# Two relative blocks: the mixture's first steps made inside the attention, the attention's parts two slots sooner, and the last batch's second normalization inside the mixture

## The reference, cut to what matters

```
x = x + 0.5 * routed_ffn(layernorm(x))        # stage 1
x = x + retention(layernorm(x))               # stage 2
x = x + 0.5 * routed_ffn(layernorm(x))        # stage 3
x = x + 0.5 * L1_ffn(layernorm(x))            # stage 4
x = x + plain_attention(layernorm(x))         # stage 5
x = x + 0.5 * L1_ffn(layernorm(x))            # stage 6

L1_ffn(src):
    x  = layernorm(src);  q, k, v = x @ wq, x @ wk, x @ wv          # 16 heads of 8
    att = softmax((q.k + q.p[relative position]) * scale)           # p = pe @ wp
    src = src + (att @ v) @ wo
    x2  = layernorm(src)
    sel = sigmoid(x2 @ sel_w)                                       # 32 experts
    gate = sel where it is among the token's top 4, else 0
    h   = relu(x2 @ keys[e]);   out = sum over e of gate[e] * (h @ values[e])
    return src + out
```

## Time and profile before

| what | us |
|---|---|
| median of 3 runs | 3079.71 (3077.35 to 3080.72) |
| the profiled execution: its own time | 3079.54 |
| its span, first to last instruction | 3077.7 |
| mean granted TensorE clock | 0.965 of 2.4 GHz |
| f4m, first issue of SP to f4m gate load | 1452.7 to 1458.2 |
| f6m, first issue of SP to the end of the span | 2696.7 to 3077.7 |

### The profile page before, as it was taken

How to read it: one execution, slowest core, us unless ns; L and a number is a source line. 1 busy time by engine, 2 the same in 40 slices (tenths; PEclk the granted TensorE clock), 3 DMA queues, 4 the chain that set the end, 5 groups by cost and what they waited for, 6 DMA issues and landing times. The chain is left out here.

```text
span 3077.7 us, 62307 instructions
## 1 busy us (share of the span) xinstructions
PE 2832.4 (92%) x21152; PEld 2287.9 (74%) x21152; DVE 1974.7 (64%) x4490; ACT 1863.7 (61%) x5065; POOL 2052.6 (67%) x2634
## 2 busy tenths in 40 slices
PE   6999798799969999997999998998999999979999
PEld 4888576588858888886788865665888888768887
DVE  5544486544448888886555556775788888755554
ACT  2233344233359999997444446776999999844444
POOL 4223574322158888884899984555788888679998
PEclk9999898899979999998999998998999999989999
DMA  3000464000022221121555546552121221055554
GB/s 112 1 1 1 104 141 102 1 1 1 1 51 42 53 53 42 43 45 46 210 191 193 193 162 127 114 117 47 43 42 43 57 49 43 22 207 200 197 195 166
DMA packets 152507, 266.08 MB, mean 86 GB/s; under 512 B 14098, under 2 KB 124946, under 8 KB 129138
## 3 DMA queue, kind: packets, MB, share of 16 engines
q1 hardware_dynamic: 152194, 262.11, 30.2%
HBM read 204.06 MB, written 53.67 MB: 84 GB/s over the span
## 5 line engine op out<-in xcount | busy, mean ns | idle before, releaser
L3005 POOL TENSOR_TENSOR f4m_ht_lo<-f4m_ht,f4m_ht_hi 128x512 fp32r<-128x512 f32 x256 | 330.6, 1309 | 36.6 <-ACT f4m_ht_hi L2941 28.5
L3005 POOL TENSOR_TENSOR f6m_ht_lo<-f6m_ht,f6m_ht_hi 128x512 fp32r<-128x512 f32 x256 | 329.8, 1303 | 31.3 <-ACT f6m_ht_hi L2941 22.0
L2980 DVE SCALAR_TENSOR_TENSOR f6m_ht<-f6m_hr,f6m_gate 128x512 f32<-128x512 f32 x256 | 176.3, 691 | 164.6 <-PE f6m_hr L2868 158.9
L2980 DVE SCALAR_TENSOR_TENSOR f4m_ht<-f4m_hr,f4m_gate 128x512 f32<-128x512 f32 x256 | 175.7, 690 | 160.2 <-PE f4m_hr L2868 149.4
L2941 ACT ACTIVATE f4m_ht_hi<-f4m_ht 128x512 fp32r<-128x512 f32 x256 | 161.3, 632 | 191.1 <-DVE f4m_ht L2980 189.5
L2941 ACT ACTIVATE f6m_ht_hi<-f6m_ht 128x512 fp32r<-128x512 f32 x256 | 161.5, 632 | 188.1 <-DVE f6m_ht L2980 188.0
L2518 ACT ACTIVATE f4a_pr<-f4a_sr,f4a_nm 128x256 f32<-128x256 f32 x512 | 241.0, 486 | 30.3 <-DVE f4a_nm L2593 30.2
L2518 ACT ACTIVATE f6a_pr<-f6a_sr,f6a_nm 128x256 f32<-128x256 f32 x512 | 241.1, 486 | 30.1 <-DVE f6a_nm L2593 30.0
L2708 POOL TENSOR_TENSOR f4a_rr<-f4a_tmp 128x256 f32<-128x256 f32 x256 | 187.2, 731 | 87.6 <-DVE f4a_tmp L2601 85.8
L2708 POOL TENSOR_TENSOR f6a_rr<-f6a_tmp 128x256 f32<-128x256 f32 x256 | 187.2, 731 | 79.3 <-DVE f6a_tmp L2601 77.2
L2601 DVE TENSOR_TENSOR f4a_tmp<-f4a_ur,f4a_turn 128x512 f32<-128x512 f32 x256 | 174.9, 684 | 67.3 <-PE f4a_ur L2378 63.9
(11 more groups left out here) (490 smaller groups left out, 9417.0 us busy)
## 6 DMA issues: line engine op xcount, KB each, us to landing
f4m_gate<-f4m_gates SPq DMA_DIRECT2D x64, 1024.0 KB, 4.6
f6m_gate<-f6m_gates SPq DMA_DIRECT2D x64, 1024.0 KB, 4.7
r_scratch<-r_parts SPq DMA_DIRECT2D x32, 192.0 KB, 2.2
all_qs<-r_scratch SPq DMA_DIRECT2D x16, 384.0 KB, 4.9
all_ks<-r_scratch SPq DMA_DIRECT2D x16, 384.0 KB, 6.7
f4al_scratch<-f4a_parts SPq DMA_DIRECT2D x32, 192.0 KB, 2.2
all_qs<-f4al_scratch SPq DMA_DIRECT2D x16, 384.0 KB, 4.8
all_ks<-f4al_scratch SPq DMA_DIRECT2D x16, 384.0 KB, 6.8
```

The lines of the kernel that those rows point to most:

```text
L2980: nc.vector.scalar_tensor_tensor(ht[:, n % RB, :], hr[:, n % HB, :], 0.0, gate[:, q % GB, n % LOADED, :], ALU.max, ALU.mult).then_inc(ht_r ...
L3005: nc.gpsimd.tensor_tensor(ht_lo[:, n % RB, :], ht[:, n % RB, :], ht_hi[:, n % RB, :], ALU.subtract)\
```

## The change

1. A class `Opening` is made once per relative block, ahead of the attention. It holds what the end of the attention and the start of the mixture share: the room for weight chunks 0 and 1, the rounded and low parts of keys chunk 0 and of the even groups' tokens, the gates' copy, the small tiles of the second normalization, and the semaphores of all of it. The mixture takes its semaphores over.
2. In the attention SP fetches chunks 0 and 1 right behind the last batch's read. In step B+1 PE turns the gates of group 0 at slot 14 into the bank of the relating products, ACT copies them at slot 15, SP stores them; POOL at slot 13 rounds keys chunk 0 and the first group's tokens (before: ACT) and makes their low part. In step B+2 DVE makes the keys' low part at slot 2.
3. The mixture starts with the gate load. ACT's first work is values chunk 0.
4. The last batch (`kept(e)` is false for it) gets no normalization from POOL's root on in the attention. The root stands at the start of POOL's list in the mixture, the normalized tokens behind ACT's first split; PE turns them behind expert 2 and selects behind expert 5; ACT takes the tokens at n = 2 and the exponential at n = 5; DVE does the five steps of the gates at n = 8, 10, 11, 13 and 14.
5. The rest of the heads moves to slot 13 of the start step, the second part to slot 15 of it, the third part to slot 1 of the prepare step. For f6's batch 1, which stage 5 has started, the first two stand at slot 0 of the prepare step.
6. For room, the odd groups' gate copy and the late batch's tokens share the tile yt (with waits that keep them apart), and the second buffer of stage 5's pts lies in the opening's chunk room.

```diff
 relative_ffn:
+        opening = Opening(nc, Pool_(nc, ctx, f"{tag}o"), f"{tag}o", k, w, io, x2t, gates)
...
 relative_attention, SP:
                 lead.read(sp, i)
+            opening.fetch(sp)                 # chunks 0 and 1, two DMAs of 512 KB
             sp.wait_ge(stacked, B * LANDED)
+            opening.store_gates(sp)
 relative_attention, PE:
-                if n == AT["x2t"] and e:
+                if n == AT["x2t"] and e and kept(e):
+                    opening.turn_tokens(pe, e[0], x2, fill(it, "x2t")).then_inc(desk.filled, 1)
+                if n == AT["sel"] and e and kept(e):
+                    opening.select(pe, x2s, fill(it, "sel")).then_inc(desk.filled, 1)
+                if n == 14 and it[0] == B + 1:
+                    pe.wait_ge(ur.emptied, 2 + B * H)
+                    opening.turn_gates(pe, ur.psum[:, 0, :])
 relative_attention, ACT:
-                if n == 3 and p:
-                    lead.second_part(act, p[0])
+                if n == 15 and b:
+                    lead.second_part(act, b[0])
+                if n == 0 and p and led and p[0] == 1:
+                    lead.second_part(act, 1)
...
+                if n == 15 and it[0] == B + 1:
+                    opening.take_gates(act, ur.psum[:, 0, :])
 relative_attention, DVE:
+                    if n == 2 and i == B - 1:
+                        opening.low_part(dve)
-                    if n == 15:
-                        gate_sum(it)
+                    if n == 15 and kept(e):
+                        dve.wait_ge(desk.emptied, desk.done(it, "sel"))
+                        opening.gate_sum(dve, i)
...
-            for n in sorted(GATES):
-                GATES[n](B - 1)
 relative_attention, POOL:
-                    if n == 1: ... lead.rest_of_heads(pool, p[0])
-                    if n == 3: lead.third_part(pool, p[0])
+                if b and n == 13:
+                    pool.wait_ge(desk.emptied, desk.done(it, "qk"))
+                    lead.rest_of_heads(pool, b[0])
+                if p and n == 0 and led and p[0] == 1:
+                    lead.rest_of_heads(pool, 1)
+                if p and n == 1:
+                    lead.third_part(pool, p[0])
+                if e and n == 7 and kept(e):
+                    opening.root(pool, e[0])
+                if n == 13 and it[0] == B + 1:
+                    opening.high_parts(pool)
 mixture, SP:
-            fetch(0)
-            fetch(1)
-            store_gates(0)
             load_gates(0)
 mixture, PE:
-            turn_gates(0)
...
+                if n == 2:
+                    opening.turn_tokens(pe, LATE, x2, turned[:, :]).then_inc(late_filled, 1)
+                if n == 5:
+                    pe.wait_ge(late_taken, 1)
+                    opening.select(pe, x2s, turned[:, :]).then_inc(late_filled, 1)
 mixture, ACT:
-            take_gates(0)
-            split_x(0)
-            split_weights(0)
             split_weights(1)
+            opening.normal(act, LATE, x2)
...
+                if n == 2:
+                    act.wait_ge(late_filled, 1)
+                    opening.take_tokens(act, LATE, x2s, turned[:, :]).then_inc(late_taken, 1)
+                if n == 5:
+                    act.wait_ge(late_filled, 2)
+                    opening.take_selection(act, LATE, turned[:, :]).then_inc(late_taken, 1)
 mixture, DVE:
-            rest_of_weights(0)
             rest_of_weights(1)
...
+                if n == 8:
+                    dve.wait_ge(late_taken, 2)
+                    opening.gate_sum(dve, LATE)
+                if n in GATES:                # {10: inverse, 11: best, 13: left, 14: kept}
+                    GATES[n](dve, LATE)
 mixture, POOL:
-            rest_of_x(0)
+            opening.root(pool, LATE)
 Opening:
+    def high_parts(self, pool):
+        pool.wait_ge(self.fetched[0], 16)
+        nc.gpsimd.tensor_copy(self.keys_hi[:, :, :], self.full[:, 0, :, :]).then_inc(self.weights_hi, 1)
+        pool.wait_ge(self.gates_ready, self.GT // TT)
+        nc.gpsimd.tensor_copy(self.x_hi ..., first).then_inc(self.x_hi_ready, 1)
+        pool.wait_ge(self.x_hi_ready, 1)
+        nc.gpsimd.tensor_tensor(self.x_lo ..., first, self.x_hi ..., ALU.subtract).then_inc(self.x_lo_ready, 1)
+    def low_part(self, dve):
+        dve.wait_ge(self.weights_hi, 1)
+        self.nc.vector.tensor_tensor(self.keys_lo[:, :, :], self.full[:, 0, :, :], self.keys_hi[:, :, :], ALU.subtract)
+    def take_tokens(self, act, i, x2s, bank):
+        for dst in (x2s, self.tiles[:, i, :]):
+            last = self.nc.scalar.activation(dst, bank[:, 0:T], ACT.Identity, scale=..., bias=...)
```

More of the change, by code:

```diff
@@ L1402, in relative_ffn @@
                 lead = Lead(nc, Pool_(nc, pair, f"{tag}l"), f"{tag}l", x_sb, k, w, io)
-                ahead(lead)
-            relative_attention(nc, f"{tag}a", x_sb, k, io, w, x2t, gates, lead)
-        mixture(nc, f"{tag}m", x_sb, k, io, x2t, gates, then, out=out)
+                ahead(lead, opening.full)
+            relative_attention(nc, f"{tag}a", x_sb, k, io, w, opening, lead)
+        mixture(nc, f"{tag}m", x_sb, k, io, x2t, gates, opening, then, out=out)
 class Forerun:
@@ L2277, in relative_attention @@
+def relative_attention(nc, tag, x_sb, k, io, w, opening, lead=None):
     x_b = x_sb[:, :, :].rearrange("p (b t) c -> p b t c", t=TT)
@@ L2339, in later_than, with kept @@
             return not isinstance(b[0], int) or b[0] >= first
+        def kept(e):
+            return e[0] < B - 1
         def run(step, ahead):
@@ L2445, in small @@
                     lead.project_heads(pe, b[0], fill(it, "qk")).then_inc(desk.filled, 1)
-                if n == AT["x2t"] and e:
-                    out = fill(it, "x2t")
-                    pe.wait_ge(x2_ready, e[0] * TT + TT)
-                    for t in range(TT):
-                        mm = nc.tensor.transpose(out[:, t * P:(t + 1) * P], x2[:, t, :], k.ident)
-                    mm.then_inc(desk.filled, 1)
-                if n == AT["sel"] and e:
-                    out = fill(it, "sel")
-                    for t in range(TT):
-                        mm = nc.tensor.matmul(out[:, t * E1:(t + 1) * E1], x2s[:, t * P:(t + 1) * P], w.selw[:, :],
-                                              start=True, stop=True)
-                    mm.then_inc(desk.filled, 1)
+                if n == AT["x2t"] and e and kept(e):
[5 more added lines that the diff above has]
+                    opening.turn_gates(pe, ur.psum[:, 0, :])
             def related(it, n):
@@ L2537, in small @@
                     lead.normal_source(act, b[0])
-                if n == 9 and e:
-                    act.wait_ge(s1_shift, e[0] + 1)
-                    for t in range(TT):
-                        nc.scalar.activation(x2[:, t, :], s1[:, t, :], ACT.Identity, scale=rstd3[:, t:t + 1], bias=nb3[:, t:t + 1])\
-                            .then_inc(x2_ready, 1)
+                if n == 9 and e and kept(e):
+                    opening.normal(act, e[0], x2)
                 if n == AT["xt"] and b:
@@ L2758, in _, with mixture @@
             run(step, shared)
-def mixture(nc, tag, x_sb, k, io, x2t, gates, then=None, out=None):
+def mixture(nc, tag, x_sb, k, io, x2t, gates, opening, then=None, out=None):
     G, GT, HB, RB, GB, SB = 8, 4, 4, 3, 2, 4
@@ L2768, in mixture @@
         a = Pool_(nc, ctx, tag)
-        full = a.sb("full", [P, SB, CHUNK, P])
-        halves = {name: (a.sb(f"{name}_hi", [P, E1, P], F32R), a.sb(f"{name}_lo", [P, E1, P], F32R))
-                  for name in ("keys", "values")}
-        (keys_hi, keys_lo), (values_hi, values_lo) = halves["keys"], halves["values"]
-        x_hi, x_lo = a.sb("x_hi", [P, 2, W], F32R), a.sb("x_lo", [P, 2, W], F32R)
+        a.sems, opening.a.sems = opening.a.sems, []
+        full = a.sb("full", [P, SB - 2, CHUNK, P])
@@ L2786, in mixture @@
+        (hr_filled, ht_ready, hi_ready, lo_ready, out_done, yt_ready, turn_done, x_done, late_filled, late_taken) = [a.sem(n) for n in (
+            "hr_filled ht_ready hi_ready lo_ready out_done yt_ready turn_done x_done late_filled late_taken").split()]
         stored = a.sem("stored")
-        fetched = [a.sem(f"fetched{n}") for n in range(SB)]
+        fetched = opening.fetched + [a.sem(f"fetched{n}") for n in range(2, SB)]
         gate_in = [a.sem(f"gate_in{n}") for n in range(GB)]
+        LATE = B - 1
@@ L2793, in mixture, with chunk_in, weights, chunk_of @@
         ORDER = {item: n for n, item in enumerate(CHUNKS)}
+        MADE = 2
+        def chunk_in(s):
+            return opening.full[:, s, :, :] if s < MADE else full[:, s - MADE, :, :]
+        def weights(name, part, e):
+            if name == "values":
+                return halves[name][part][:, e, :]
+            return (opening.keys_hi, opening.keys_lo)[part][:, e, :] if e < CHUNK else halves[name][part][:, e - CHUNK, :]
+        def chunk_of(name, part, c):
+            first = c - (CHUNK if name == "keys" else 0)
```

(7 more changed lines are left out.)

233 lines of the change are left out of this document (140 added, 93 removed).

## The result

The changed kernel takes 3056.39 us (median of 5 runs, 3054.97 to 3065.12), the kernel before in the same measurement 3080.27 us (3077.35 to 3083.13): ratio 0.9933 (this kernel's time over that of the kernel before), 95% interval 0.992 to 0.9946, which leaves out 1. The profiled execution has a span of 3054.2 us against 3077.7. So 23.5 us went, where 28.0 were forecast.

What follows compares the result with a forecast made beforehand. PE, busy 92% of the span, was taken as the bound, so only its waits and low-clock time could go. Moved parts -10.7 us, opening and late batch -17.3: together -28.0 from 3079.54, so 3051.5 us, range 3046 to 3057.

Steps and rivals of the forecast that it cites:

- Waits for stacks: In both attentions, PE's slot 11 waits for stacked heads all go: 5.45 us in f4, 6.10 in f6.
- A clean step stays 34.25: Attention steps without long PE waits keep 34.25 us, since idle time on POOL and ACT takes up the moved parts.
- Rivals 2, 3 and 5: 2: ACT slot 15 too full, 3064, 0.07; 3: lighter steps, 3043, 0.06; 5: POOL slot 13 delays terms, 3101, 0.02.
- The fill of f4: At f4's start batch 0's third part stands behind batch 1's root on POOL: 0.9 us later, bounds 0 to 1.5.
- Taken off the path, 24.1: Between attention and mixture, late-batch work and gate and key preparation leave the path: 12.2 us in f6, 11.9 in f4.
- 0.6 per block in the last steps: In the attention's last steps ACT's gates' copy adds 0.6 us per block, bounds 0 and 2.6.
- Rival 4: Gates reach memory late, with SP behind its waits for landed stacks; 5.44 us per block stay: 3062, chance 0.03.
- The first group, 2.8 per block: In the mixture's first group, added ACT and DVE work costs 2.8 us per block, bounds 0.5 and 4.6.
- Other edits cost nothing: Value chunk 0's split and rest stand beside the gate load; the other attention's second buffer only changes address: 0 us.
- rival 1: The opening gives half back: longer low clock, first group and last steps at upper prices; 3062.5, chance 0.12.

Runs made afterwards that it cites:

- the run without it: The changed kernel with the last batch's second normalization, turns and gates back in the attention, none of it in the mixture; ratio 0.9972 to the kernel before.
- the 224 bytes: The changed kernel with 224 unused bytes per partition behind the opening's tiles, bringing the mixture's tiles back to byte 160 of 256; ratio 0.9914 to the kernel before.
- the second measurement: The changed kernel itself, measured once more on another chip: 3058.4 us, ratio 0.9943 to the kernel before.

## Why the forecast held, and where it missed

- **Waits for stacks: right in mechanism, short in f6.** They are gone in every step. Thirteen steps of f4 are 5.9 us shorter (forecast 5.45), fourteen of f6 7.4 us (forecast 6.10). The forecast took 34.25 us for each of the fourteen, but the first of them needs only 33.4 where nothing waits, so the waits in f6 were more than it read. In timed runs the parts are worth less than in these traces: 5 us (2 to 8) alone and 7, with some 5 of doubt, when taken back. "A clean step stays 34.25": 34.24, by the place of the tiles. Rivals 2, 3 and 5 did not come: ACT's slot 15 and POOL's slot 13 carry the moved parts without a longer step.
- **The fill of f4: 0.9 forecast, 1.0 in this pair, but 1.6 over all traces** (nine with the new slots 68.5 to 69.5 us from PE's first instruction to the third batch's product for v, five with the old ones 67.2 to 67.8): above the upper bound of 1.5. The forecast put the cost ahead of PE's first relating product. Behind that product the stretch takes 48.6 to 48.8 us with the new slots and 47.6 to 47.9 with the old, 1.0 us that the forecast does not have; ahead of it 0.7 us come on average. Which instruction takes it was not followed.
- **Taken off the path, 24.1, less 0.6 per block in the last steps: right.** 22.9 us forecast, 23.2 measured. DVE closes batch 14's gates 0.69 and 0.66 us later, counted from PE's product for v of batch 15; the rest is gone. The late batch is 6.5 and 6.8 of it, the opening 5.2 and 4.7. Rival 4 did not come.
- **The first group, 2.8 per block: too dear.** The late batch costs 1.2 to 1.5 us by the run without it. Opening and late batch together cost 1.7 us by the averages above, and 0.9 by the pair of traces (1.7 less the place's 0.8); the stretch itself varies by 2 us between traces of kernels that are alike in it. The sum took ACT's and DVE's added work in full up to product 13, as in a serial loop. That a part of it lay beside other work is the likely reason, but not shown.
- **The failed step: "Other edits cost nothing".** The forecast says there that a moved buffer "only changes its address", and it has no term at all for where the tiles of the mixture lie: the tokens' tiles of the even groups and the first keys' tiles now begin at byte 160 of 256, all the others at 192. These places cost 3.13 us in the six periods of each block and 0.8 in its first group. With the 224 bytes these 7.8 us go. Between the two traces the mixtures differ by 8.7 us, since f6's last group took 1.35 us longer in the changed kernel's first trace than in its second.

The 4.5 us between forecast and trace are thus: periods +6.3, last groups +1.8, parts with both fills +1.5 (the clock in f6's start in it), first groups -2.2, last steps and passages -0.3, and ahead of f4 -2.6. A price that was too high and a higher clock ahead of f4 hid more than half of what the places cost. So that 3056.39 lies in the forecast's range, 0.6 us below its upper end, is in part luck. By the second measurement's ratio the kernel would stand at 3062 us (3058 to 3066), above the range. That is near rival 1's 3062.5, but rival 1's mechanism, a slower opening, is not what the runs show. The range itself is narrower than the bounds it names: added in full they give 3045 to 3060.

Not settled: what in the chip makes products slower. Shown is only this dependence, for float32r products of 512 columns with weights loaded beside them: an expert's six products take 1.36 us where tokens, keys, values and hidden layer all begin at the same byte of 256, and some 0.03 us more where one of them does not. It is not enough that the two operands of a product agree. In an even group's first eight experts tokens and keys both begin at byte 160, values and hidden layer both at 192, and the expert takes 1.39 us all the same. Here the products before and after read from the other place. Whether it is the tokens streamed against the next product's weights loaded meanwhile was not tried.

## What to carry to other kernels

When a tile moves to another allocation, compare the addresses of all that neighbouring matmuls of the loop read, not only of the two operands of one: here 224 unused bytes took 7.8 us out of the two mixtures. Compare PE's period in steady state before and after, even where nothing waits, and before an edit is blamed for a stretch in which the granted clock is low, see how much that stretch varies between traces of one kernel. A wait of 4 us on an engine off the path is worth nothing until PE's own wait behind it is.

## What the runs showed of the hardware

- With the tokens 64 or 128 bytes within 256 from weights and hidden layer, a group of 32 experts takes 1.01 to 1.09 us more, some 2.3%; 256 and 1024 bytes away, nothing. With the tokens 32 and the hidden layer 64 bytes from the weights it is 1.01 us too.
- The attention's step takes 34.27 us with its first tile at byte 160 of 256 (the run with 224 bytes), 34.24 at byte 192, 34.19 at byte 224 (the run with 32 bytes behind the opening) and 34.155 at byte 0.
- Two traces of one program differ by 5.6 us at one point, 860 us in, with a granted clock of 0.95 against 0.94 up to there. Two traces of the same instructions differ by 1.8 us in f6's start, with a clock of 0.52 against 0.92 in 8 us of it.
- 1 MB of fetches issued right behind a read of 384 KB on one queue left its landing at 6.6 to 7.5 us, against 6.3 to 6.9 without them: 0.2 us on average.
